# Four chained image layers on one core: gate spread by transposes, key context as four 32-column heads, full 128x128 products for layer 1, a third buffer for exponentials, and new written orders

## The reference

```
# layer 0: nearest code of 1024, decoded
dis = sum(xf*xf) + sum(E*E) - 2*xf@E ; idx = argmin(dis) ; out = E.T[idx]
# layer 1: attention inside each 64-token row, sigmoid for softmax
f = x@Wf + bf ; g = x@Wg + bg ; h = x@Wh + bh          # 32, 32, 256 channels
out = sigmoid(f g^T) @ h                               # 64x64 scores per image row
# layer 2: one number per token
x0, x1, x2 = x.w1 + b1, x.w2 + b2, x.w3 + b3           # n = 4096 each
sm = softmax(x0[:, None] * x1[None, :], axis=1) ; feats = x2 @ sm
out = sigmoid(feats) * x
# layer 3: linear attention, 4 heads of 32
q, k, v = split(x@w_qkv) ; q = softmax over channels * 32**-0.5 ; k = softmax over tokens
context[h] = k[h] v[h]^T  (32x32) ; out = LN(context^T q @ w_out + b_out)*gamma + beta
```

## Time and profile before

| | |
|---|---|
| timed runs | 5932.96, 5922.93, 5923.11 us; median 5923.11 |
| the profiled execution's own time | 5934.16 us, span 5932.2 us |
| PE busy | 5488.0 us, 93% of the span |
| DVE busy | 4208.7 us, 71% |
| ACT busy | 3968.5 us, 67% |
| POOL busy | 1920.9 us, 32% |
| mean granted TensorE clock | 0.947 |
| chain that ended last | PE 68%, DVE 15%, ACT 11%, issue 5%, POOL 1% |

### The profile page before, as it was taken

How to read it: one execution, slowest core, us unless ns; L and a number is a source line. 1 busy time by engine, 2 the same in 40 slices (tenths; PEclk the granted TensorE clock), 3 DMA queues, 4 the chain that set the end, 5 groups by cost and what they waited for, 6 DMA issues and landing times.

```text
span 5932.2 us, 110733 instructions
## 1 busy us (share of the span) xinstructions
PE 5488.0 (93%) x42728; PEld 2905.2 (49%) x42728; DVE 4208.7 (71%) x8970; ACT 3968.5 (67%) x6129; POOL 1920.9 (32%) x1588
## 2 busy tenths in 40 slices
PE   5799999999999999999999999999999999999976
PEld 2425546364553645446363544636455363544514
DVE  6547677776777777677776767777677777767615
ACT  1266767677675767767577676767767576676763
POOL 2314233242423424242342423334142342424312
PEclk8899999999999999999999999999999999999966
DMA  2010110102011020101102010010201101010000
GB/s 72 14 32 16 58 29 23 56 9 66 21 54 33 12 64 13 62 25 47 39 6 69 15 59 28 31 51 7 67 21 58 29 12 64 13 61 26 19 11 29
DMA packets 163161, 211.04 MB, mean 36 GB/s; under 512 B 13136, under 2 KB 146000, under 8 KB 162640
## 3 DMA queue, kind: packets, MB, share of 16 engines
q1 hardware_dynamic: 138064, 136.82, 7.1%
q0 software_dynamic: 24576, 67.14, 3.9%
HBM read 136.80 MB, written 67.11 MB: 34 GB/s over the span
## 4 chain that ended last, share of the span: by engine, by line
PE 68%; DVE 15%; ACT 11%; issue 5%; POOL 1%; DMA 0%; SPq 0%; DVEq 0%; ACTq 0%; POOLq 0%
PE PS L1029 33%; PE PS L1195 12%; PE PS L1186 5%; ACT big L544 4%; DVE stats L743 3%; PE PS L1129 3%; PE PS L1080 2%; DVE XT L791 2%; PE PS L1288 2%; PE PS L1058 2%; ACT n_x L478 2%; PE PS L1261 1%; PE PS L1096 1%; ACT o_x L478 1%; DVE yout L959 1%
## 5 line engine op out<-in xcount | busy, mean ns | idle before, releaser
L544 ACT ACTIVATE big<-PS 128x1024 f32<-128x1024 f32 x2048 | 1994.9, 1024 | 1022.6 <-PE PS L1186 714.9
L1195 PE MATMUL PS<-big,w 128*4 128x512 f32 x8192 | 1115.3, 633 | 5.9 <-ACT big L544 4.0
L391 POOL DMA_INDIRECT quant_H<-emb_t,idx x512 | 487.7, 952 | 1135.6 <-DVE idx L767 925.2
L1029 PE MATMUL PS<-e_hi,n_hi 128*128 128x512 f16 x2048 | 784.4, 383 | 19.0 <-DVE m L761 11.2
L1029 PE MATMUL PS<-e_lo,n_hi 128*128 128x512 f16 x2048 | 780.1, 381 | 0.0
L1029 PE MATMUL PS<-e_hi,n_lo 128*128 128x512 f16 x2048 | 779.2, 380 | 0.0
L743 DVE BATCH_NORM_STATS2 stats<-XT 128x6 f32<-128x512 f32 x1024 | 652.9, 683 | 18.7 <-POOL XT L407 9.4
L1186 PE MATMUL PS<-rhs,lhs 12*128 12x512 bf16 x4096 | 549.0, 400 | 81.9 <-ACT big L544 61.9
L767 DVE FIND_INDEX8 idx<-m,work 128x8 uint32<-128x1024 f32 x512 | 623.2, 1219 | 0.0
L761 DVE CUSTOM_DVE_ANT_0 work<-PS,e_bias,m 128x512 f32<-128x512 f32 x512 | 383.7, 749 | 250.4 <-PE PS L1029 244.9
L761 DVE CUSTOM_DVE_ANT_0 work<-PS,e_bias 128x512 f32<-128x512 f32 x512 | 347.9, 679 | 265.2 <-PE PS L1029 264.6
(11 more groups left out here) (212 smaller groups left out, 10914.3 us busy)
## 6 DMA issues: line engine op xcount, KB each, us to landing
xin<-x SPq DMA_DIRECT2D x128, 512.0 KB, 3.9
out<-yout SPq DMA_DIRECT2D x128, 512.0 KB, 2.9
quant_H<-emb_t,idx POOLq DMA_INDIRECT x512, 2.7
XT<-emb SPq DMA_DIRECT2D x1, 1024.0 KB, 4.9
XT<-wh SPq DMA_DIRECT2D x1, 256.0 KB, 4.9
XT<-wqv SPq DMA_DIRECT2D x1, 256.0 KB, 5.2
XT<-wk SPq DMA_DIRECT2D x1, 128.0 KB, 5.2
w_sb<-w SPq DMA_DIRECT2D x1, 128.0 KB, 5.0
```

What stands on the lines that cost most here:

```text
L391: nc.gpsimd.indirect_dma_start(quant[:, g % 2, u, :], None, emb_t, bass.IndirectOffsetOnAxis(ap=idx[:, t % (2 * GT), 0:1], axis=0),).then_ ...
L544: nc.scalar.activation(E[:, h % 2, z * 1024:(z + 1) * 1024], bank(2 * z, 2), ACT.Exp).then_inc(exped.sem, 1)
L1029: ins = mm(dst, a, b, start=first and j == 0, stop=last and j == 2)
L1195: ins = mm(PS[32 * q:32 * q + 4, 4, :], w2[:, t, f, :], E[:, h % 2, q * 512:(q + 1) * 512], start=h == 0, stop=h == HALVES - 1, skip_group ...
```

## The change

- `spread` is four transposes a group in place of four fp32 products.
- `l3_ctx` makes for each of the four blocks four products, one a head: 128 rows by 32 columns of keys, 32 columns of values, each into its own 32 PSUM partitions. `ctxg`, `ctxf` and the copy of L908 are 32 columns wide.
- `attn` is 128 columns wide for each block, set to zero once at the start. `l1_tanh` writes only the two 64x64 blocks on its diagonal, with two instructions of 64 partitions in place of each one of 128. `l1_out` makes full 128x128 products, channels 0 to 127 into bank 7 and the others into bank 6, with a semaphore step after each; DVE adds each bank with one instruction of 512 columns.
- `E` has a third buffer, in half of `soft`, where the layer 3 keys `ke` and `kt` lie at other times. The first use of it in a turn waits for the last `l3_ctx` of the image before. `squares` moves from there to `o_hi`.
- The lists of steps of all engines but SP are written anew. By the lists, TensorE changes the shape of the array 238 times a turn before and 225 times after: 191 to 174 in the exponential stretch, 40 to 33 in the layer 1 stretch, 7 to 18 in the layer 3 stretch.

```diff
-        attn = sb("attn", [P, 2, GT, ROW])
+        attn = sb("attn", [P, 2, GT, P])
-        E = big[:, :].rearrange("p (s n) -> p s n", s=2)
+        E = [big[:, 0:2048], big[:, 2048:4096], soft[:, 2048:4096]]
+        squares = o_hi[:, :, :, :].rearrange("p s k n -> p (s k n)").bitcast(F32).rearrange("p (u c) -> p u c", u=GT)
+        ctxg = yout[:, 1, 0, :].rearrange("p (g e) -> p g e", g=NG)
             def l1_tanh(im, g):
-                nc.scalar.activation(pairs, PS[:, 4, 0:GT * ROW], ACT.Tanh, scale=0.5)
+                for r in range(2):
+                    rr = slice(r * ROW, (r + 1) * ROW)
+                    last = nc.scalar.activation(attn[rr, g % 2, :, rr],
+                                                PS[rr, 4, 0:GT * ROW].rearrange("p (u i) -> p u i", u=GT), ACT.Tanh, scale=0.5)
...
-                nc.scalar.activation(pairs, pairs, copy, bias=ones[:, 0:1])
+                for r in range(2):
+                    last = nc.scalar.activation(attn[rr, g % 2, :, rr], attn[rr, g % 2, :, rr], copy, bias=ones[rr, 0:1])
             def exp(im, h, z):
-                    act.wait_ge(*summed.room(im, h, 2))
+                    act.wait_ge(*summed.room(im, h, 3))
+                    if h == 2 and im > 0:
+                        act.wait_ge(*l3_ctxed.after(im - 1, NG - 1))
             def l1_out(im, g):                       # DVE
                 for k in range(KC):
-                    for r in range(2):
-                        here = XT[:, im % 2, k, g, :].rearrange("p (u r i) -> p u r i", u=GT, r=2)[:, :, r, :]
-                        made = PS[:, 6 + r, k * GT * ROW:(k + 1) * GT * ROW].rearrange("p (u i) -> p u i", u=GT)
+                    here = XT[:, im % 2, k, g, :]
+                    dve.wait_ge(*l1_outed.after(im, 2 * g + k))
+                    v.scalar_tensor_tensor(out=here, in0=bank(7 - k), scalar=beta_c[:, k:k + 1], in1=here, op0=ALU.add,
+                                           op1=ALU.add).then_inc(l1_added.sem, 1)
             def l1_out(im, g):                       # PE
                 for k in range(KC):
                     for u in range(GT):
-                        for r in range(2):
-                            ins = mm(PS[:, 6 + r, (k * GT + u) * ROW:(k * GT + u + 1) * ROW],
-                                     H[rr, g % 2, u, k * P:(k + 1) * P], attn[rr, g % 2, u, :], start=True, stop=True)
+                        ins = mm(PS[:, 7 - k, u * P:(u + 1) * P], H[:, g % 2, u, k * P:(k + 1) * P], attn[:, g % 2, u, :],
+                                 start=True, stop=True)
+                    ins.then_inc(l1_outed.sem, 1)
             def spread(im, g):
-                    ins = mm(PS[:, g % 2, u * P:(u + 1) * P], gate[:, 2, t:t + 1].broadcast_to([P, P]), ident[:, :],
-                             start=True, stop=True)
+                    ins = tr(PS[:, g % 2, u * P:(u + 1) * P], gate[:, 2, t:t + 1].broadcast_to([P, P]), ident[:, :])
             def l3_ctx(im, g):                       # PE
-                    ins = mm(PS[:, ctx_bank(g), 0:P], kt[:, g % 2, u, :], V[:, g % 2, u, :], start=u == 0, stop=u == GT - 1)
+                    for h in range(HEADS):
+                        hh = slice(h * DH, (h + 1) * DH)
+                        ins = mm(PS[hh, ctx_bank(g), 0:DH], kt[:, g % 2, u, hh], V[:, g % 2, u, hh], start=u == 0,
+                                 stop=u == GT - 1, skip_group_check=True)
             for new, old, last in images(B):         # PE, exponential stretch, two places
-                fill(old, 16, 0); fill(old, 16, 1); sums(old, 15)
-                final_z(last, 8); final_out(last, 6); fill(old, 17, 0); fill(old, 17, 1); sums(old, 16)
+                final_out(last, 6); fill(old, 16, 1); final_z(last, 8); turn_in(new, 5); fill(old, 17, 0)
+                fill(old, 17, 1); sums(old, 15)
+                sums(old, 16)
...
-                score(new, 8, 1); sums(old, 38)
-                sums(old, 39)
+                score(new, 8, 1); turn0(new, 2); fill(old, 39, 0); fill(old, 39, 1); sums(old, 36)
+                sums(old, 37)
+                sums(old, 38)
...
```

More of the change, by code:

```diff
@@ L649, in _ @@
+                exp(old, 50, 0); l0_norm(new, 7, 0); l0_norm(new, 7, 1); gated(old, 0); exp(old, 50, 1)
+                exp(old, 51, 0); exp(old, 51, 1); exp(old, 52, 0); l0_norm(new, 7, 2); l0_norm(new, 7, 3)
                 exp(old, 52, 1); exp(old, 53, 0); exp(old, 53, 1); exp(old, 54, 0); exp(old, 54, 1)
@@ L1332, in _ @@
-                turn_in(new, 11); final_z(last, 15); fill(old, 25, 0); final_out(last, 13); fill(old, 25, 1)
+                l3_kturn(last, 7); fill(old, 0, 0); fill(old, 0, 1); fill(old, 1, 0); fill(old, 1, 1)
+                l3_ctx(last, 7); fill(old, 2, 0); sums(old, 0)
+                fill(old, 2, 1); fill(old, 3, 0); l3_qturn(last, 6); sums(old, 1)
+                fill(old, 3, 1); combine(last, 1); fill(old, 4, 0); combine(last, 2); fill(old, 4, 1)
+                sums(old, 2)
+                fill(old, 5, 0); fill(old, 5, 1); final_z(last, 0); sums(old, 3)
@@ new lines, in _ @@
+                sums(old, 9)
+                fill(old, 12, 0); final_z(last, 5); sums(old, 10)
+                fill(old, 12, 1); fill(old, 13, 0); sums(old, 11)
+                final_out(last, 3); turn_in(new, 2); fill(old, 13, 1); fill(old, 14, 0); sums(old, 12)
+                final_z(last, 6); final_out(last, 4); turn_in(new, 3); fill(old, 14, 1); fill(old, 15, 0)
+                sums(old, 13)
+                final_z(last, 7); final_out(last, 5); turn_in(new, 4); fill(old, 15, 1); fill(old, 16, 0)
@@ L1333, in _ @@
                 sums(old, 24)
[L1334 removed]
+                fill(old, 26, 0); final_out(last, 14); turn_in(new, 13); fill(old, 26, 1); fill(old, 27, 0)
                 sums(old, 25)
[L1336 to L1338 removed]
@@ new lines, in _ @@
+                sums(old, 62)
+                sums(old, 63)
+                gate_chain(old, 0); l1_fg(new, 0); l1_h(new, 0, 0); spread(old, 0); l1_h(new, 0, 1)
+                spread(old, 1); l1_scores(new, 0); spread(old, 2); l1_h(new, 1, 0); l1_h(new, 1, 1); l1_fg(new, 1)
+                l1_out(new, 0); spread(old, 3); l1_scores(new, 1); l1_h(new, 2, 0); l1_h(new, 2, 1); l1_fg(new, 2)
+                l1_out(new, 1); l1_scores(new, 2); l1_h(new, 3, 0); spread(old, 4); spread(old, 5)
+                l1_h(new, 3, 1); l1_fg(new, 3); l1_out(new, 2); l1_scores(new, 3); spread(old, 6); spread(old, 7)
```

400 lines of the change are left out of this document (186 added, 214 removed).

## The result

The changed kernel takes 5869.03 us in the median (four runs, 5863.68 to 5884.38), the kernel before 5923.16 beside it: a ratio of 0.991 (0.989 to 0.993), 54 us less, where 140 us less were forecast (5783 us, from 5685 to 5885). The time lies inside the range; the direction was right and the size was not.

What follows compares the result with a forecast made beforehand. TensorE, busy 93% of the span, bounds the kernel. Layer 1 -2.5, layer 3 -2.3 and exponentials -4.3 make -9.1 us an image, 146 us in 16, less 6 for the first: 5783 us, range 5685 to 5885.

Steps and rivals of the forecast that it cites:

- the layer 1 stretch: Layer 1: TensorE saves 4.3 us, ACT rises to 57.6; stretch put at 63.2 us, -2.5 (+2 to -4.3).
- the gate's spread: Layer 1: transposes instead of fp32 products save TensorE 0.456 us a group, 3.65 us an image.
- signs of being wrong: Layer 1 window not shrinking, a low-clock stretch appearing inside it, or the exponentials' window moving by more than 9 us.
- Rival E: Slower by the clock: TensorE waiting for ACT's tanh in layer 1 may drop to 1.2 GHz; 6024 us, chance 0.08.
- Exponentials: Exponential stretch: 0.64 us for the eighth context, 1.63 for shapes, 2.0 of idle time; -4.3 us (0 to -9).
- Layer 3: Layer 3 stretch: 3.45 us off TensorE, with DVE at 44.2 of 55.0; taken as -2.3 us (0 to -3.5).
- the head products: Key context: 32-column products run four side by side, 0.25 us a group instead of 0.90; saves 5.15 us an image.
- The first image: Layer 1 of the first image has no old image, so ACT's longer chain lies bare; 6 us taken back.
- B: Key context's head products go one after another, 0.99 us a group; 5872 us, chance 0.12.
- C: ACT and DVE hide TensorE's gains in layers 1 and 3, exponentials' idle time stays; 5860 us, chance 0.14.
- D: More goes than counted: low-clock time and half the exponentials' remaining idle time; 5681 us, chance 0.13.
- F: New lists wait where the old did not and eat the gain; within 0.2% of 5923 us, chance 0.06.

Runs made afterwards that it cites:

- e2: Kernel after, with ACT making only one of the two halves of layer 1's tanh and add of 1 (not a usable version): 5776.80 us, 0.975.
- e8: Kernel after, with one tanh a group into a scratch and only the add of 1 in halves, on ACT: 5824.13 us, 0.984.
- e5: Kernel before, with the gate spread by transposes as the only change: 5923.40 us, 1.000.
- e11: Kernel after, with e8's one tanh and e13's later first spread together: 5769.72 us, 0.974.
- e14: e11 with the gate spread as fp32 products again instead of transposes: 5802.92 us, 0.980.
- e13: Kernel after, with only an image's first spread moved one step later in TensorE's list: 5817.18 us, 0.983.
- e10: Kernel after, with the old lists of steps for the exponential stretch: 5858.57 us, 0.989.
- e4: Kernel before, with the third buffer for exponentials alone, old lists: 5940.23 us, 1.003.
- e6: Kernel before, with the key context as 32-column head products alone: 5904.77 us, 0.997.
- e3: Kernel before, with the new layer 1 outputs alone (full products, tanh and add in halves), old lists: 5929.90 us, 1.001.
- e7: Kernel after, with all parts of the change but all of the old lists of steps: 5928.81 us, 1.002.
- e1: Kernel after, with the old layer 1 outputs (half products, one tanh, four DVE adds), new lists kept: 5905.34 us, 0.997.
- e15: e11 with the old lists of steps for the exponential stretch: 5811.21 us, 0.982.
- e16: e11 with the gate's add of 1 moved from DVE to ACT: 5789.43 us, 0.978.
- e9: Kernel after, with one tanh on ACT and its add of 1 given to DVE in halves: 6088.22 us, 1.028.

## Why the direction was right and the size wrong

**The failed step** is the one on the layer 1 stretch: "The two become equally long with a chain between them, so neither can be full: I put the stretch at 63.2, -2.5 us". It measured 67.7, +0.8. I had ACT's load nearly right (57.6, measured 59.0) and also that it meets TensorE's, and then took 4.3 us off TensorE, gave 1.8 back for the chain, and called it a gain. The clock in this stretch I left as it was. What the runs show: the stretch follows ACT at about 0.75 us a us (e2, e8), about a third of it through the clock, so ACT's halves cost 92 us to the full and 45 us in the part that one tanh avoids. The 3.65 us of the gate's spread, which I counted in full on TensorE's side, are worth 0.6 us on the old lists (e5) and 2.3 in e11 (e14). The slack that I counted on was real, 7.5 us of waiting for the scores, but as I read it, it stood between ACT's instructions and was not free for the chain of f and g, scores, tanh, add, output. Two of my signs of being wrong came: the layer 1 window did not shrink, and low time appeared inside it.

**A wait I did not price** is the first spread's. The gate needs 5.2 us from the first product of its chain: in the trace of before the chain starts at 3335.96 and its last DVE operation ends at 3341.16, after 3307.03 and 3312.21. Before, TensorE came to the spread at 3341.62 and did not wait, since the clock was low at the start of the stretch and most of f, g and h ran at half speed:

```profile
3341.06 0.40 PE L1029 MATMUL PS<-h_hi,n_lo 128*128 128x256 f16 x1
3341.27 0.29 PE L1029 MATMUL PS<-h_hi,n_hi 128*128 128x256 f16 x1
...
3341.62 1.06 PE L1213 MATMUL PS<-ident,gate 128*128 128x128 f32 x8
```

After, it comes early, waits 1.96 us and then runs slow. I had read the low clock at the start as a loss and not seen that it covered a latency. It cost 52 us (e13), 40 of them in the two profiled executions.

**The clock.** Rival E named this mechanism for layer 1, "if TensorE there waits for ACT's longer tanh group by group, it may fall", with too large a size: low time behind ACT's copy is there in 13 of 15 images, and low time behind the gate's wait, which E did not name, in the same 13. Before, the stretch was not at full clock "but for its first 3.4 us" either; the mean is 6.6 us, 5.2 of it at the start. That went when the others came, so layer 1 has only 0.5 us more. Low time went up by 3.4 us an image in all, half of which is 1.7 us or 27 us in 16 images, and 3.0 of the 3.4 are in the exponentials, of which E says nothing. The forecast had it unchanged. e11 goes down by 5.2 us instead. The 32 more transposes an image did not bring the low clock: e11 has them and no low time in layer 1, and e14 with products in their place has 1.6 us.

**Exponentials**, forecast -4.3, measured -1.6. The net is -3.1, and 1.5 us of it went to 3.0 us more low time. The terms of my sum (0.64 for the eighth context, 1.63 for the shapes, 2.0 of idle time) were not measured one by one. With the old exponential lists the net is 217.4 us, as before (e10), so the new products and the third buffer bring nothing here, and the new order of steps brings the 3.0. ACT's wait for `sums` fell from 18.0 us to 3.7 (and 0.3 for `soft`), as forecast, and it was worth nothing by itself (e4); a part of it is now a wait for a `fill`, 49.9 us where it was 46.5:

```profile
ACT big L552 <- PE PS L1190: 26.5, 23, 4.1
...
ACT soft L552 <- PE PS L1190: 23.4, 13, 7.9
...
ACT big L552 <- PE PS L1199: 3.7, 2, 1.9
...
PE PS L1190 <- ACT big L552: 2.1, 4, 0.7
```

TensorE's own waits for exponentials are no less than before: 2.1 us here, 0.5 for those in `soft` and 1.1 at a `sums`, against 2.2. Hence the buffer by itself did not bring the 3.0 us, and the lists did; whether they could without the buffer that they are laid out for, no run shows.

**Layer 3**, forecast -2.3, measured -3.0: near in size, but not by the head products alone, to which I gave it all. On the old lists they give 0.5 (e6, 55.1 to 54.6), the new layer 1 outputs, at which I had put nothing here, give 1.9 (e3, 53.2; DVE is busy 41.9 us in the stretch in place of 44.1, ACT waits 1.7 us for `kneg` in place of 4.1), and all parts together 2.7 (e7, 52.4). The new lists add 0.3 to that. With the new lists but the old outputs it is 2.5 (e1, 52.6). So the head products count beside the new lists or the new outputs and little alone, no run takes them out of the kernel after, and that the size came near is in part luck.

**The first image.** The 6 us that I took back for it did not come: up to its gate it is 0.2 us longer than before, and no run shows that term.

**Rivals.** B (the heads one after another, 5872 us) has nearly the measured time and is wrong: 0.26 us a group. C (gains hidden by ACT and DVE in the first two stretches, idle time of the third staying, 5860 us) comes nearest in time with a mechanism that is there: ACT in layer 1. It is wrong on layer 3, which gave 3.0 us where C has 1. D's low clock did not go in the kernel after but did in layer 1 of e11. F is ruled out by the ratio.

**What stays open**: why the new lists bring 3 to 5 us more low time an image in the exponential stretch (after, e11) than the old ones (e10, e15), and what of the layer 1 stretch is ACT's load and what the length of the chain through it. e16's longer wait and e4's 16 us are open too.

## What to carry to other kernels

Where one engine's saved time and another's added time meet in one stretch, don't net them: move the load off the engine that rises (one tanh instead of two) and test that alone. Before pricing a faster step, look for the latency that the slow step was covering, and put work of its own length ahead of the next wait; here the order of two steps in one list was worth as much as everything the change brought. Savings of single parts say little when the order of the work is written out: four parts came to +6 us on the old lists and to -54 us on lists made for them.

## What the runs showed of the hardware

A small DVE operation between SBUF and SBUF can take ten times its length beside POOL. The gate's add of 1 on 32 columns takes 0.18 us at its shortest, in the last image, and 2.15 us in the median (ns least, median, most; first and last start; then the two engines at one such place in the trace of the kernel before):

```profile
L857 DVE TENSOR_SCALAR gate<-gate x16: 181/2151/2155, 524.5 to 5701.4; 128x32 f32<-128x32 f32 x16
```

```profile
3338.60 2.13 POOL L401 TENSOR_TENSOR n_lo<-n_x,n_hi 128x1024 f16<-128x1024 f32 x1 [0.91 <-ACT n_hi L508]
3338.61 2.16 DVE L852 TENSOR_SCALAR gate<-gate 128x32 f32<-128x32 f32 x1 [1.02 <-ACT gate L558]
```

POOL starts 0.01 us ahead, and DVE ends 0.04 us behind it; its record holds the time it was held up. Such a row looks busy and is for the most part a wait. In 15 of 16 images of both kernels POOL starts first, by about 0.01 us; in the last no POOL operation runs beside it, and it takes 0.18 us. The Trainium skill, "SBUF — State Buffer", the section "SBUF: two separate sides", says that DVE in some modes and POOL share a port pair under an exclusive lock, and the one that comes second is blocked for the other's whole instruction. By that rule DVE ends by its own 0.18 us behind POOL; the trace agrees on the hold-up, with 0.04 us behind here and 0.15 in e9's pair. No row shows which mode DVE is in.

Short products on different 32-column parts of the array start 8 ns apart (0.26 us for 32, in the first timeline row above), where the Trainium skill's "TensorE: Matmul & The Clock Gate" has about 25 ns as the closest (section "Wait — 56ns, not 53.3ns?"). The rule does not hold across parts of the array here, as the prediction took from `fill`.

TensorE's longest wait for ACT's copy in layer 1 was followed within 2 us by 1.2 GHz in some images and not in others: a wait of 1.34 us in 0 of 15 (e11), of 1.44 in 9 (e16), of 1.63 in 9 (e8), of 1.89 in 14 (e13), of 2.15 in 13 (after). In e16 TensorE is idle 5.4 us of the stretch and in e11 5.6, so it was the longer single wait and not the sum that went with low time there; what decides it in a given image the runs don't show. With the spread one step later (e13) the stretch lost 0.6 us net and 3.9 us of low time.
